# GpSimd computes four of the eight parts of the final sum of a transformer block, VectorE the other four

## The chip, the cores and the metric

The kernel runs on one core of one Trainium2 chip. The metric is the device time of one execution in microseconds (us), lower being better. The compute engines of a core are TensorE (PE), VectorE (DVE), ScalarE (ACT) and GpSimd (POOL); SyncE (SP) only issues DMAs here. They run their own instruction streams and are ordered by semaphores.

## The reference, cut to what matters

The input x has 2 x 1024 rows of 128 float32 numbers. The output is x plus causal attention of the normalised rows plus a mixture of experts, in which each row takes the two best of 16 experts:

```python
xn = _layernorm(x, axis=-1)
x = x + _L0_attn_ref(xn, Wk, bk, Wq, bq, Wv, bv) + _L0_ffn_ref(xn, Wr, br, W1, b1, W2, b2)
# inside _L0_ffn_ref
gate = jnp.sum(jax.nn.one_hot(topi, NUM_BANKS) * topv[..., None], axis=-2)
h = jax.nn.relu(jnp.einsum('bsd,edh->bseh', tensor, W1) + b1)
y = jnp.einsum('bseh,ehm->bsem', h, W2) + b2
out = jnp.einsum('bse,bsem->bsm', gate, y)
```

What concerns the change is the last sum: every output row is a partial result (x, attention and the gated b2) plus gate 0 times the first expert's vector plus gate 1 times the second's.

## The kernel before, in words

The 2048 rows are 16 tiles (NT) of 128 rows, one row for each partition. `xin` (128 x 16 x 128, float32, in SBUF) starts as x and collects the output in place. The stages, in the order of time:

1. Rows are normalised and the router picks two experts for each; GpSimd scatters the rows to DRAM, sorted by expert (L361), in 47 tiles (TILES). L363 is a memset of a scratch tile between these scatters.
2. Attention of tiles 0 to 12 (the last three, `LATE`, wait until the end). For each tile VectorE adds the causal mask and takes the row maximum (L621), ScalarE exponentiates (L433), TensorE transposes (L847) and multiplies with v (L867), and VectorE adds the result to `xin` (L640), which raises `o_read`.
3. The 47 expert tiles: TensorE's two layers (L970 to L972, L982), ScalarE's ReLU (L473), VectorE's rescale into `ybuf` (L701), and an indirect DMA from the GpSimd queue that scatters each result to `pairs_dram` (L369), two vectors for each row of the input.
4. SyncE waits until the 47 scatters have landed (L313) and loads `pairs_dram` back in eight parts (NYL = 8) of two tiles each (TYL = 2), 256 KB a part (L315). Meanwhile the attention of tiles 13, 14 and 15 runs.
5. VectorE finishes the attention, waits for `o_read` to be 16, and runs `combine(n)` for n from 0 to 7. Each part is four `scalar_tensor_tensor` instructions on 128 x 128 (L724), two tiles for k = 0, a wait on its own semaphore (`step`), and two tiles for k = 1: `xin` = `pairs` x gate + `xin`. Both tensors are in SBUF. The last one raises `res_done`.
6. SyncE waits for `res_done` to be n + 1, in the order of n, and sends part n of `xin` to the output, 128 KB (L319). When all eight have landed the kernel ends.

The `pairs` tile lies in the same SBUF memory as the tile that the trace calls `slots`, so the rows of the trace call it `slots`. GpSimd's stream before the change ends with the 47 scatters (L365 to L371).

In L724 the operand of the gate is one number for each partition, `gate[:, k, t:t + 1]`. In front of GpSimd's engine, `step` (L326) makes it wait on its own semaphore, as VectorE's does.

The functions around the change:

Of the kernel before, what the change touches and what calls it, by code (L numbers as in the profile page):

```python
# [5 lines left out]
ALU = mybir.AluOpType  # L6
# [12 lines left out]
def attention_and_top2_experts(nc, x, Wk, bk, Wq, bq, Wv, bv, Wr, br, W1, b1, W2, b2, out):  # L19
# [3 lines left out]
    K = 2  # L23
    NT = B * S // P
# [19 lines left out]
    NYL = 8  # L44
    TYL = NT // NYL
# [7 lines left out]
    with ExitStack() as ctx:  # L53
        def sb(name, shape, dt):
            return ctx.enter_context(nc.sbuf_tensor(name, shape, dt))

        def sem(name):
            return ctx.enter_context(nc.semaphore(name))

        xin = sb("xin", [P, NT, D], F32)  # L60
# [57 lines left out]
        gate = sb("gate", [P, K, NT], F32)  # L118
# [12 lines left out]
        pairs = flat_slots[:, 0:NT * K * D].rearrange("p (t k d) -> p t k d", k=K, d=D)  # L131
# [57 lines left out]
        pairs_in = [sem(f"pairs_in{n}") for n in range(NYL)]  # L189
# [51 lines left out]
        o_read = sem("o_read")  # L241
# [4 lines left out]
        relu_done = sem("relu_done")  # L246
        l2_done = sem("l2_done")
        y_done = sem("y_done")
        res_done = sem("res_done")

        x_v = x.rearrange("b (t p) d -> p (b t) d", p=P)
        out_v = out.rearrange("b (t p) d -> p (b t) d", p=P)
# [21 lines left out]
        @block.sync  # L274
        def _(sp):
            def load_x(g):
                sp.dma_start(xin[:, G * g:G * g + G, :], x_v[:, G * g:G * g + G, :]).then_inc(x_in[g], 16)

            load_x(0)
            load_x(1)  # L280
            sp.dma_start(wr[:, :], Wr).then_inc(router_in, 16)
            load_x(2)
            sp.dma_start(brb[:, :], br.rearrange("(a e) -> a e", a=1).broadcast_to([P, E])).then_inc(router_in, 16)
            load_x(3)
            for n, w in enumerate((Wq, Wk, Wv)):
                sp.dma_start(wqkv[:, n, :], w).then_inc(proj_in, 16)
            sp.dma_start(bqk[:, 0:1], bq.rearrange("(p a) -> p a", a=1)).then_inc(proj_in, 16)
            sp.dma_start(bqk[:, 1:2], bk.rearrange("(p a) -> p a", a=1)).then_inc(proj_in, 16)
            sp.dma_start(b1rows[0:E, :], b1).then_inc(b1_in, 16)
            sp.wait_ge(blank_made, 1)  # L290
            whole = TILES // NBL * NBL
            blank_i = blank.bitcast(I32)
            sp.dma_start(blank_v[:, 0:whole, :].rearrange("p (m n) c -> p m (n c)", n=NBL),
                         blank_i.rearrange("p n c -> p (n c)")[:, None, :].broadcast_to([P, TILES // NBL, NBL * ROW])
                         ).then_inc(blank_sent, 16)
            sp.dma_start(blank_v[:, whole:TILES, :], blank_i[:, 0:TILES - whole, :]).then_inc(blank_sent, 16)
            sp.dma_start(bvb[:, :], bv.rearrange("(a d) -> a d", a=1).broadcast_to([P, D])).then_inc(bias_in, 16)
            for n in range(NW):
                here = slice(WG * n, WG * n + WG)
                sp.dma_start(w1[:, here, :], w1_v[:, here, :]).then_inc(w1_in[n], 16)  # L300
            sp.dma_start(b2rows[0:E, :], b2).then_inc(b2_in, 16)
            for n in range(NW):
                here = slice(WG * n, WG * n + WG)
                sp.dma_start(w2[:, here, :], w2_v[:, here, :]).then_inc(w2_in[n], 16)

            sp.wait_ge(proj_done, 3 * NG)
            sp.wait_ge(gates_done, 1)
            sp.wait_ge(rows_sent, 16 * K * NT)
            for n, (a, z) in enumerate(zip(XG, XG[1:])):
                sp.dma_start(slots_i[:, a:z, :], slots_v[:, a:z, :]).then_inc(slots_in[n], 16)  # L310

            for n in range(NYB):
                sp.wait_ge(y_sent[n], 16 * len(range(n, TILES, NYB)))  # L313
            for n in range(NYL):
                sp.dma_start(pairs[:, TYL * n:TYL * n + TYL, :, :],  # L315
                             pairs_v[:, TYL * n:TYL * n + TYL, :, :]).then_inc(pairs_in[n], 16)
            for n in range(NYL):
                sp.wait_ge(res_done, n + 1)
                sp.dma_start(out_v[:, TYL * n:TYL * n + TYL, :], xin[:, TYL * n:TYL * n + TYL, :]).then_inc(out_sent, 16)  # L319
            sp.wait_ge(out_sent, 16 * NYL)  # L320

        @block.gpsimd
        def _(pool):
            made = [0]

            def step(ins):  # L326
                made[0] += 1
                ins.then_inc(pool_step, 1)
                pool.wait_ge(pool_step, made[0])

            pool.memset(epsc[:, :], EPS)
            pool.memset(blank, 0.0)
            step(pool.memset(ident[:, :], 0.0))
            pool.affine_select(out=ident[:, :], in_=ident[:, :], compare_op=ALU.not_equal, fill=1.0,
                               base=0, pattern=[[-1, P]], channel_multiplier=1).then_inc(ident_made, 1)
            pool.iota(blank.bitcast(I32)[:, :, D:D + 1], pattern=[[0, NBL], [0, 1]], base=LOST,
                      channel_multiplier=0).then_inc(blank_made, 1)
            pool.iota(rows_i[:, :, D:D + 1], pattern=[[K * P, NT], [0, 1]], base=0, channel_multiplier=K)
            step(pool.iota(expert_no_i[:, :], pattern=[[1, E]], base=0, channel_multiplier=0))
            pool.tensor_copy(expert_no[:, :], expert_no_i[:, :])  # L340
            pool.memset(ones[:, :], 1.0)
            pool.memset(keep[:, :, 1:NT], 1.0)
            pool.memset(keep[:, :, 0:1], 0.0)
            pool.memset(ones16[:, :], 1.0 / P)
            step(pool.memset(before[:, :], 1.0))
            pool.affine_select(out=before[:, :], in_=before[:, :], compare_op=ALU.is_gt, fill=0.0,
                               base=0, pattern=[[1, P]], channel_multiplier=-1)
            step(pool.iota(tileno_i[:, :], pattern=[[0, 1]], base=0, channel_multiplier=1))
            pool.tensor_copy(tileno[:, :], tileno_i[:, :]).then_inc(consts, 1)
            step(pool.memset(causal[:, :], 0.0))  # L350
            pool.affine_select(out=causal[:, S - P:], in_=causal[:, S - P:], compare_op=ALU.is_ge, fill=-HUGE,
                               base=0, pattern=[[-1, P]], channel_multiplier=1).then_inc(consts, 1)

            pool.wait_ge(blank_sent, 32)
            pool.wait_ge(xn_done, NG)
            pool.wait_ge(slotrow_done, 1)
            for k in range(K):
                if k == 1:
                    pool.wait_ge(slotrow_done, 2)
                for t in range(NT):  # L360
                    pool.indirect_dma_start(slots_dram, bass.IndirectOffsetOnAxis(ap=slotrow[:, k, t:t + 1], axis=0),  # L361
                                            rows_i[:, t, :], None).then_inc(rows_sent, 16)
                    step(pool.memset(tick[:, :], 0.0))  # L363

            for j in range(TILES):  # L365
                if j in XG:
                    pool.wait_ge(pair_done, XG.index(j) + 1)
                pool.wait_ge(y_done, j + 1)
                pool.indirect_dma_start(pairs_dram, bass.IndirectOffsetOnAxis(ap=pair[:, j:j + 1], axis=0),  # L369
                                        ybuf[:, j % NYB, :], None, bounds_check=NT * P * K - 1,  # L370
                                        oob_is_err=False).then_inc(y_sent[j % NYB], 16)  # L371

        @block.scalar
        def _(act):
# [105 lines left out]
        def _(dve):  # L480
            made = [0]

            def step(ins):
                made[0] += 1
                ins.then_inc(dve_step, 1)
                dve.wait_ge(dve_step, made[0])
# [233 lines left out]
            def combine(n):  # L720
                dve.wait_ge(pairs_in[n], 16)
                for k in range(K):
                    for t in range(TYL * n, TYL * n + TYL):
                        ins = dve.scalar_tensor_tensor(out=xin[:, t, :], in0=pairs[:, t, k, :],  # L724
                                                       scalar=gate[:, k, t:t + 1], in1=xin[:, t, :], op0=ALU.mult,
                                                       op1=ALU.add)
                    if k + 1 < K:
                        step(ins)
                ins.then_inc(res_done, 1)

            attention(NT - LATE, NT)
            dve.wait_ge(o_read, NT)
            for n in range(NYL):
                combine(n)

        @block.tensor
# [290 lines left out]
```

## Time and profile before

| what | value |
|---|---|
| median of 3 runs | 206.0 us (205.99 to 206.23) |
| the profiled execution, its own time | 205.87 us |
| its span, first to last instruction | 204.1 us |
| busy: PE, DVE, ACT, POOL | 165.2, 115.0, 113.3, 100.0 us |
| TensorE's mean granted clock | 0.915 |

The profiled execution has 1.77 us outside its span. Busy time is an average over stages with different limits; what a stage depends on is read from the chain of waits and from the timeline of its stretch. A line of the timeline has the start, the duration, the engine, the line of the kernel, the operation, output <- input, the shape (partitions x elements), the count, and in brackets the idle time before it with what ended it. Durations of single instructions overlap somewhat with their neighbours on an engine, so the distance between two starts can be shorter than one duration.

### The profile page before, as it was taken

What the parts mean: (1) busy time and instruction counts of PE and PEld (TensorE: products, weight loads), DVE (VectorE), ACT (ScalarE), POOL (GpSimd) and SP (SyncE); (2) the same over time, 40 slices, a digit from 0 to 9 for tenths busy, and PEclk for the clock granted to TensorE, in tenths of its full rate; (3) what the DMA queues carried; (4) which work ended last, traced back from release to release, by engine and by line L of the source; (5) the groups of instructions that cost most, each with busy time, mean ns of one, the idle gap of its engine ahead of it and who ended that gap; (6) DMA issues with size and microseconds to landing.
All of it is one profiled execution on the core that took longest, in us unless ns stands there. A gap on an engine that the chain in (4) does not pass through costs nothing.

```text
span 204.1 us, 4590 instructions
## 1 busy us (share of the span) xinstructions
PE 165.2 (81%) x1464; PEld 146.3 (72%) x1464; DVE 115.0 (56%) x429; ACT 113.3 (56%) x325; POOL 100.0 (49%) x133
## 2 busy tenths in 40 slices
PE   5777999588989879205999999999998999988600
PEld 5667448446688578104999999999998999947500
DVE  3717777666979754303676644454444344354595
ACT  0885279268889582001988666656666666536000
POOL 7000008888888888840155545555555455640000
PEclk9995599999999999555999999999999999999975
DMA  5899999921011101129901100000100000007533
GB/s 158 281 323 181 385 408 409 408 82 39 29 42 39 39 29 39 39 53 303 279 29 43 38 29 37 18 11 39 42 31 24 28 30 32 24 0 242 174 103 103
DMA packets 22102, 23.69 MB, mean 116 GB/s; under 512 B 2689, under 2 KB 15515, under 8 KB 22080
## 3 DMA queue, kind: packets, MB, share of 16 engines
q1 hardware_dynamic: 19552, 19.16, 30.2%
q0 software_dynamic: 2528, 4.24, 6.0%
q8 instruction: 13, 0.21, 0.4%
q14 instruction: 9, 0.07, 0.1%
HBM read 14.98 MB, written 9.39 MB: 119 GB/s over the span
## 4 chain that ended last, share of the span: by engine, by line
PE 49%; POOL 24%; DVE 9%; ACT 6%; issue 6%; DMA 4%; DVEq 0%; SPq 0%; POOLq 0%; ACTq 0%
PE pO L982 21%; POOL slots_dram L361 15%; POOL tick L363 8%; PE pS L970 6%; PE pS L972 5%; PE pS L971 5%; DVE xin L724 4%; ACT rows L385 3%; PE pS L765 3%; PE pT L940 3%; PE pO L867 2%; PE pS L832 1%; PE pO L757 1%; DMA slots<-slots_dram 1%; DMA xin<-in_L_attn_x 1%
## 5 line engine op out<-in xcount | busy, mean ns | idle before, releaser
L473 ACT ACTIVATE xT<-pS,b1t 128x128 f32<-128x128 f32 x188 | 53.6, 372 | 40.8 <-PE pS L972 40.8
L369 POOL DMA_INDIRECT pairs_dram<-ybuf,pair x47 | 46.2, 983 | 46.4 <-DVE ybuf L701 41.4
L982 PE MATMUL pO<-w,xT 128*128 x376 | 51.7, 282 | 0.0
L361 POOL DMA_INDIRECT slots_dram<-rows,slotrow x32 | 32.3, 1010 | 34.1 <-DVE slotrow L563 25.5
L982 PEld LDWEIGHTS pO<-w,xT 128*128 128x128 f32 x376 | 45.5, 192 | 0.0
L693 DVE CAST xT<-pT 128x128 f16<-128x128 f32 x47 | 13.7, 291 | 44.8 <-PE pT L940 43.9
L970 PE MATMUL pS<-xT,w1hi 128*128 128x128 f16 x188 | 35.0, 223 | 2.4 <-DVE xT L694 1.9
L971 PE MATMUL pS<-xT,w1hi 128*128 128x128 f16 x188 | 35.0, 223 | 0.0
L972 PE MATMUL pS<-xT,w 128*128 128x128 f16 x188 | 35.0, 223 | 0.0
L970 PEld LDWEIGHTS pS<-xT,w1hi 128*128 x188 | 21.6, 115 | 3.4 <-DVE xT L694 2.5
L971 PEld LDWEIGHTS pS<-xT,w1hi 128*128 x188 | 21.6, 115 | 0.1
L972 PEld LDWEIGHTS pS<-xT,w 128*128 x188 | 21.6, 115 | 0.0
L940 PE MATMUL pT<-ident,slots 128*128 128x128 f32 x47 | 13.2, 286 | 8.7 <-DMA slots<-slots_dram 8.7
L867 PEld LDWEIGHTS pO<-v,probsT 128*128 128x128 f32 x144 | 17.7, 192 | 3.0 <-issue 1.4
L867 PE MATMUL pO<-v,probsT 128*128 128x128 f32 x144 | 18.9, 279 | 1.1 <-DVE wscale L609 1.1
L433 ACT ACTIVATE probs<-pS,negm 128x128 f32<-128x128 f32 (+7 forms) x16 | 11.9, 742 | 12.4 <-DVE negm L621 12.4
L832 PE MATMUL pS<-kT,qT 128*128 128x512 f32 (+3 forms) x48 | 17.9, 489 | 0.8 <-DVE v L585 0.8
L701 DVE TENSOR_SCALAR ybuf<-pO,cf 128x128 f32<-128x128 f32 x47 | 16.1, 343 | 3.2 <-PE pO L982 3.1
L363 POOL MEMSET tick<- 128x512 f32 x32 | 17.3, 540 | 0.0
L847 PE MATMUL pT<-ident,probs 128*128 128x128 f32 x72 | 10.9, 279 | 5.0 <-ACT probs L433 5.0
L694 DVE TENSOR_TENSOR xT<-pT,xT 128x128 f16<-128x128 f32 x47 | 13.7, 292 | 1.6
L621 DVE CUSTOM_DVE_ANT_0 pS<-pS,causal 128x128 f32<-128x128 f32 (+7 forms) x16 | 12.1, 762 | 4.1 <-PE pS L832 4.1
(125 smaller groups left out, 233.4 us busy)
## 6 DMA issues: line engine op xcount, KB each, us to landing
w<-in_L_ffn_W SPq DMA_DIRECT2D x8, 1024.0 KB, 14.8
slots_dram<-slots SPq DMA_DIRECT2D x1, 2860.0 KB, 13.5
slots<-pairs_dram SPq DMA_DIRECT2D x8, 256.0 KB, 5.7
slots<-slots_dram SPq DMA_DIRECT2D x1, 1495.0 KB, 13.3
xin<-in_L_attn_x SPq DMA_DIRECT2D x4, 256.0 KB, 3.1
out<-xin SPq DMA_DIRECT2D x8, 128.0 KB, 1.8
slots<-slots_dram SPq DMA_DIRECT2D x1, 780.0 KB, 7.3
pairs_dram<-ybuf,pair POOLq DMA_INDIRECT x47
```

The lines of the kernel that those rows point to most:

```text
L361: pool.indirect_dma_start(slots_dram, bass.IndirectOffsetOnAxis(ap=slotrow[:, k, t:t + 1], axis=0), rows_i[:, t, :], None).then_inc(rows_s ...
L363: step(pool.memset(tick[:, :], 0.0))
L369: pool.indirect_dma_start(pairs_dram, bass.IndirectOffsetOnAxis(ap=pair[:, j:j + 1], axis=0), ybuf[:, j % NYB, :], None, bounds_check=NT * ...
L473: ins = nc.scalar.activation(hid[:, j % NHB, here], pA(j)[:, here], ACT.Relu, bias=b1t[:, c, j:j + 1])
L701: dve.tensor_scalar(ybuf[:, j % NYB, :], pO[j % 2][:, 0:D], cf[:, j:j + 1], None, ALU.mult).then_inc(y_done, 1)
L832: ins = pe.matmul(pS[t % 2][:, a:z], qT[:, t * P:(t + 1) * P], kT[:, at + a:at + z], start=True, stop=True)
L867: ins = pe.matmul(pO[t % 2][:, 0:D], probsT[t % 2][:, j // G, j % G * P:(j % G + 1) * P], v[:, t // TB * TB + j, :], start=(j == 0), stop= ...
L940: pe.transpose(pT[j % 2][:, 0:D], slots[:, j, 0:D], ident[:, :]).then_inc(xs_done, 1)
L970: pe.matmul(to, w_hi, x_hi, start=True, stop=False)
L971: pe.matmul(to, w_hi, x_lo, start=False, stop=False)
L972: ins = pe.matmul(to, w_lo, x_hi, start=False, stop=True)
L982: ins = pe.matmul(pO[r % 2][:, 0:D], hid[:, r % NHB, c * P:(c + 1) * P], second_weights(r, c), start=(c == 0), stop=(c == NCH - 1))
```

## The change

VectorE's `combine` runs for the odd parts only. The even parts are computed by GpSimd, after its last scatter: for a part it waits for the pairs and for `o_read` of the part's two tiles, multiplies four 128 x 128 blocks of `pairs` in place by their gates (`tensor_scalar`), adds the two halves (`tensor_tensor`, 128 x 256), and adds the sum to `xin` (`tensor_tensor`, 128 x 256). A wait on its own semaphore stands between the three steps. `res_done` becomes two semaphores, and SyncE waits for one or the other in the order of n. Indices of `o_read`: parts 0, 2, 4 and 6 need it at 2, 6, 10 and 14.

```diff
-        res_done = sem("res_done")
+        res_dve = sem("res_dve")
+        res_pool = sem("res_pool")
...
             for n in range(NYL):
-                sp.wait_ge(res_done, n + 1)
+                if n % 2:
+                    sp.wait_ge(res_dve, n // 2 + 1)
+                else:
+                    sp.wait_ge(res_pool, n // 2 + 1)
                 sp.dma_start(out_v[:, TYL * n:TYL * n + TYL, :], xin[:, TYL * n:TYL * n + TYL, :]).then_inc(out_sent, 16)
...
+            for n in range(0, NYL, 2):
+                pool.wait_ge(pairs_in[n], 16)
+                pool.wait_ge(o_read, min(TYL * n + TYL, NT))
+                for k in range(K):
+                    for t in range(TYL * n, TYL * n + TYL):
+                        ins = pool.tensor_scalar(pairs[:, t, k, :], pairs[:, t, k, :], gate[:, k, t:t + 1], None,
+                                                 ALU.mult)
+                step(ins)
+                step(pool.tensor_tensor(pairs[:, TYL * n:TYL * n + TYL, 0, :], pairs[:, TYL * n:TYL * n + TYL, 0, :],
+                                        pairs[:, TYL * n:TYL * n + TYL, 1, :], ALU.add))
+                pool.tensor_tensor(xin[:, TYL * n:TYL * n + TYL, :], xin[:, TYL * n:TYL * n + TYL, :],
+                                   pairs[:, TYL * n:TYL * n + TYL, 0, :], ALU.add).then_inc(res_pool, 1)
...
-                ins.then_inc(res_done, 1)
+                ins.then_inc(res_dve, 1)
 
             attention(NT - LATE, NT)
             dve.wait_ge(o_read, NT)
-            for n in range(NYL):
+            for n in range(1, NYL, 2):
                 combine(n)
```

## Rows read from the trace of the kernel before

**Rows 1.** The chain that ended last, 191 to 204 us: start, duration, what.

```profile
190.90 1.02 PE pO L867 x9
...
192.01 0.36 DVE xin L640
192.37 0.02 issue
192.39 0.63 DVE xin L724 x2
193.02 0.02 issue
193.04 1.15 DVE xin L724 x4
...
198.92 1.15 DVE xin L724 x4
...
201.27 0.35 DVE xin L724
201.62 0.26 DVEq L53
```

**Rows 2.** One line's instructions, L724: durations in ns, first and last start.

```profile
L724 DVE SCALAR_TENSOR_TENSOR xin<-slots,gate,xin x32: 346/346/352, 192.4 to 201.5; 128x128 f32<-128x128 f32 x32
```

**Rows 3.** One line's instructions, L319, the output's DMAs, and their landing.

```profile
L319 SPq DMA_DIRECT2D out<-xin x8: 372/372/378, 193.7 to 201.9; - x8
DMA to landing us min/median/max: 1.8/1.8/1.8
```

**Rows 4.** The timeline of SyncE's queue, 178 to 205 us.

```profile
183.02 5.15 SPq L315 DMA_DIRECT2D slots<-pairs_dram  x8
193.68 8.60 SPq L319 DMA_DIRECT2D out<-xin  x8
```

**Rows 5.** L315 in short stretches: single loads of parts 0, 2 and 7; parts 6 and 7.

```profile
L315 SPq DMA_DIRECT2D slots<-pairs_dram x1: 359/359/359, 183.0 to 183.0; - x1
DMA to landing us min/median/max: 2.7/2.7/2.7
...
L315 SPq DMA_DIRECT2D slots<-pairs_dram x1: 463/463/463, 183.9 to 183.9; - x1
...
DMA to landing us min/median/max: 5.4/5.4/5.4
...
L315 SPq DMA_DIRECT2D slots<-pairs_dram x1: 1674/1674/1674, 186.5 to 186.5; - x1
DMA to landing us min/median/max: 6.4/6.4/6.4
...
L315 SPq DMA_DIRECT2D slots<-pairs_dram x2: 469/1072/1674, 186.0 to 186.5; - x2
...
DMA to landing us min/median/max: 6.3/6.3/6.4
```

**Rows 6.** L640 in the late attention, tiles 13 to 15, 187 to 193 us.

```profile
189.20 0.34 DVE L640 SCALAR_TENSOR_TENSOR xin<-pO,rinv,xin 128x128 f32<-128x128 f32 x1
```

**Rows 7.** The timeline of POOL, its last scatter, and its first 6 us.

```profile
180.76 0.98 POOL L369 DMA_INDIRECT pairs_dram<-ybuf,pair  x1 [0.30 <-issue]
...
3.45 0.29 POOL L346 TENSOR_SCALAR_AFFINE_SELECT slots<-slots 128x128 f16<-128x128 f16 x1
3.70 0.12 POOL L348 IOTA tileno_i<- 128x1 int32 x1
```

**Rows 8.** Groups of instructions of POOL by line: busy us, mean ns | idle before.

```profile
L334 POOL TENSOR_SCALAR_AFFINE_SELECT ident<-ident 128x128 f32<-128x128 f32 x1 | 0.3, 282 | 0.2 <-POOL ident L333 0.2
L363 POOL MEMSET tick<- 128x512 f32 x32 | 17.3, 540 | 0.0
L341 POOL MEMSET ones<- 128x128 f32 x1 | 0.2, 198 | 0.0
```

**Rows 9.** Groups of instructions of DVE by line and shape.

```profile
L561 DVE TENSOR_TENSOR slots<-slots 128x256 f32<-128x256 f32 x2 | 0.8, 420 | 0.0
L520 DVE TENSOR_TENSOR slots<-expert_no,slots 128x128 f32<-128x128 f32 x4 | 1.0, 285 | 0.0
L615 DVE SCALAR_TENSOR_TENSOR w<-w,wscale,w1hi 128x512 f16<-128x512 f32 x16 | 11.8, 746 | 0.0
```

**Rows 10.** The timelines of DVE and of POOL around 45 us.

```profile
44.67 0.56 DVE L607 TENSOR_SCALAR expo<-expo 128x4 int32<-128x4 int32 x1
45.27 0.17 DVE L608 TENSOR_SCALAR pw<-expo 128x4 int32<-128x4 int32 x1
...
44.66 0.54 POOL L363 MEMSET tick<- 128x512 f32 x1
```

**Rows 11.** The timeline of DVE around L615, beside POOL's memsets and scatters.

```profile
54.66 0.79 DVE L615 SCALAR_TENSOR_TENSOR w<-w,wscale,w1hi 128x512 f16<-128x512 f32 x1
```

## The prediction, written before the change was timed

> **What bounds the kernel now.** I read the chain that ended last first. Its tail is not TensorE: PE's last product ends at 191.9 us, L640 adds it to `xin`, and from 192.39 to 201.88 the chain is nothing but L724 on VectorE, all 32 instructions with gaps of 0.02 us [rows 1]. One part of the sum takes 1.175 us: (201.88 + 0.02 - 192.39) / 8 = 1.19 with its own waits, and 1.15 + 0.02 = 1.17 from the lines of four instructions. One L724 lasts 0.346 us [rows 2], and four of them would be 1.38, so neighbours overlap by 0.05 each. Next I read what follows: the last output DMA is issued at 201.9 and lands 1.8 later [rows 3], and the span ends at 204.1, 2.2 us after that issue. So the end is the issue of the last output DMA plus 2.2, and that issue waits for the last part.
>
> Then I asked when the inputs of the parts are there. SyncE issues the eight loads of pairs from 183.02 on [rows 4]. Part 0 lands 2.7 after 183.0, at 185.7; part 2 at 183.9 + 5.4 = 189.3; part 6 at 186.0 + 6.3 = 192.3 and part 7 at 186.5 + 6.4 = 192.9 [rows 5]. The loads between land about 0.7 apart, part 4 at about 190.9. `o_read` reaches 14 when tile 13 is added, 189.20 + 0.34 = 189.5 [rows 6], which is before GpSimd can come to part 6, so no `o_read` holds GpSimd back. GpSimd's last scatter ends at 181.7 [rows 7], so GpSimd is free when part 0 lands.
>
> **What the change removes.** Four of eight parts leave VectorE: 4 x 1.175 = 4.70 us. If nothing disturbs it, VectorE does parts 1, 3, 5 and 7 from 192.39 to 197.09.
>
> **What it adds: a part on GpSimd.** The trace has no `tensor_scalar` and no `tensor_tensor` on POOL.
> - Four multiplications of 128 x 128. The nearest row is the affine select of the same 128 columns, one input and one output: 0.282 us [rows 8], with 0.25 from its start to the next instruction's [rows 7]. I take 3 x 0.25 + 0.28 = 1.03 us. Bounds: below, a memset of that size, 0.2 each; above, 0.5 each, since the multiplication also fetches a gate for each partition, which no row shows.
> - Two additions of 128 x 256 with two inputs. Below, VectorE's own 0.42 us for that shape [rows 9]; above, two memsets of 512 columns, 2 x 0.54 = 1.1 [rows 8]. From 128 to 512 columns the memset grows by (540 - 198) / 384 = 0.89 ns a column; 512 columns fetched are 0.46, and the fixed part of the affine select is 0.28 - 0.11 = 0.17, together 0.63. A memset neither fetches nor adds, so I take 0.7.
> - Two waits on its own semaphore and one on SyncE's data: between 0.07 and the 0.24 that stood in front of the affine select; 0.1 each [rows 8].
>
> One part: 1.03 + 2 x 0.7 + 3 x 0.1 = 2.7 us, with ends at 1.8 (0.7 + 0.84 + 0.2) and 4.4 (2.0 + 2.2 + 0.2).
>
> The Trainium skill (GPSIMD Engine Reference, section 3.1) gives about 2.6 cycles at 1.2 GHz an element for a two-input addition on GpSimd. By that 256 columns would be an estimated 0.55 us plus the dispatch, and the sum would not move by more than 0.2 us.
>
> **GpSimd's line without any disturbance.** Part 0 runs from 185.7 to 188.4; part 2 from its landing at 189.3 to 192.0; part 4 to 194.7; part 6 to 197.4. Two parts thus run while VectorE is still in the attention, and cost nothing there: in that stretch VectorE reads PSUM and at most one SBUF tensor (L621, L631, L640), and TensorE, which sets the end of the attention, doesn't wait on GpSimd. The other two run beside VectorE's four.
>
> **SyncE's queue.** It sends in the order of n. Part 0 goes at about 188.5, right after the last L315 has left the sequencer at 188.2 [rows 4]; then it stands waiting for part 1, which VectorE has at 193.6. Nothing else is in that queue. The 128 KB of part 0 may push the loads still in flight by about 0.4 us; part 4 is needed 1.1 after it lands and part 6 2.4 after, so this costs nothing. If parts 6 and 7 are ready together, the last DMA is issued 0.37 later, for the issue before it [rows 3]. I count 0.2.
>
> **Both engines on SBUF at once.** This is the term that decides. At 44.67 a VectorE instruction on 4 columns lasts 0.56 us, while its neighbour of the same kind takes 0.17; GpSimd's memset started at 44.66 and lasted 0.54 [rows 10]. It looks as if VectorE stood still for the whole of GpSimd's instruction. On the other hand L615, which like L724 reads two SBUF tensors, takes 0.73 to 0.79 us beside the same memsets (mean 0.746 [rows 9], for example [rows 11]), so it is not held up by a GpSimd instruction that only writes. No row has L724's kind beside a GpSimd instruction that reads.
>
> The Trainium skill (SBUF — State Buffer, section "Who interferes with whom") speaks against this change: a VectorE instruction with two SBUF inputs and a GpSimd instruction that reads SBUF exclude one another, and the second one is blocked until the first is done. The trace agrees as far as it goes, in that the 4-column instruction was blocked and L615 was not. By that rule taken to the letter the time would be that of the second rival below.
>
> In the shared stretch VectorE has 4.7 us of work, and GpSimd has 2 x 2.7 less what it did before 192.39, 5.0 us; 9.7 together. If they exclude each other only while data flow: VectorE grows by (420 - 285) / 128 = 1.05 ns a column [rows 9], 16 x 0.135 = 2.2 us; GpSimd has 8 x 0.11 + 4 x 0.46 = 2.7. That is half of 9.7 and leaves room, though each will often find the other in its way. I bound the cost by nothing (parts end at 197.4) and by all in turn (192.39 + 9.7 = 202.1, and 0.8 more if L724's overlap of 4 x 0.05 a part is lost as well, 202.9 at most) and take the middle: the last part is there at 200.0, its DMA is issued at 200.2, against 201.9 now. That is 1.7 us sooner.
>
> **The sum.** The profiled execution took 205.87 us, a span of 204.1 and 1.77 around it, 0.13 below the median of 206.0. 205.87 - 1.7 = 204.2, and against the median 206.0 - 1.7 = **204.3 us**.
>
> **The rivals.**
> - *The two engines don't disturb each other.* For it: L615 was not disturbed [rows 11]. Against it: [rows 10]. The last part is then part 6 at 197.4, and part 7 goes 0.4 later, at 197.8, 4.1 sooner than now: 201.9. With a GpSimd part at 1.8 VectorE's 197.1 would be last: 201.2.
> - *They take turns in full*, the rule above: everything from 192.39 on is one queue of 9.7 us, which ends at 202.1 instead of 201.88, or at 202.9, plus 0.2 for the output: 0.4 to 1.2 slower, 206.4 to 207.2, **slower**, say 206.8. It decides the sign once turns add more than about 4.5 us to the 197.4. For it speaks that a blocked VectorE instruction waited out the whole memset [rows 10]. In the profile L724 would show 0.5 to 1 us in place of 0.346.
> - *GpSimd is simply too slow.* With a part at 4.4 its parts would end at 190.1, 194.5, 198.9 and 203.3, and with the output's issue the kernel ends 1.8 later than now: 207.8, also slower. The point from which this decides is a part of (201.5 - 185.7) / 4 = 3.95 us. For it: no row shows either operation on POOL. Against it: the affine select is as fast as a VectorE instruction of that size.
>
> **How the numbers follow.** Partial disturbance, my forecast: 0.43, with a range of its own of 202.7 to 205.9. No disturbance: 0.17. Turns in full: 0.26. GpSimd too slow: 0.14. A measurement of this kernel can tell 0.2%, 0.4 us, from no change. Faster are the first case but for 0.03 at its upper end, all of the second and a little (0.04) of the others, where turns in full meet a cheap GpSimd part: 0.61. Within 0.4 us: the upper end of the first and the lower end of the third and fourth, 0.12. Slower: 0.27. The range that leaves out 2 in 10 goes from 201.4, which takes in most of the undisturbed case, to 207.2, the dear end of turns in full; the slow GpSimd beyond it is left out.
>
> **What the profile of the changed kernel would show.** POOL's `tensor_scalar` at 0.28 and `tensor_tensor` at 0.7 us; part 0 ready at 188.4 and part 2 at 192.0; before 192.4 everything on PE, ACT and DVE as now. After it, L724 longer than 0.346, by how much being the disturbance: 16 of them end at 197.1 if there is none, at 202 or later if turns are full. The last line of the chain may be VectorE or GpSimd. The forecast is wrong if L724 stays at 0.346, if the GpSimd instructions cost more than 0.5 and 1.1 us already before 192.4, where nothing disturbs them, or if PE's last product moves away from 191.9.

## The result, and the profile after

The changed kernel took **210.95 us** (median of 4 runs, 209.81 to 211.13) against 206.0 (205.96 to 206.23): ratio 1.0227, 95% interval 1.019 to 1.0263. That is 5 us slower; forecast were 1.7 us faster, in a range that ended at 207.2. The profiled execution took 210.95 us, with a span of 209.2 against 204.1, so the 5 us are in the span. Medians here are of all runs of a kernel, while the ratios leave out runs in a second, slower state of the chip, so the two need not agree to the last tenth.

First the part whose parts the prediction priced, the timeline of the changed kernel from 186 us on (GpSimd's and VectorE's lines of the sum, and SyncE's; L383, L386, L388 are GpSimd's three steps, L742 is the old L724, L658 the old L640, L323 the old L319):

```profile
186.03 2.35 POOL L383 TENSOR_SCALAR slots<-slots,gate 128x128 f32<-128x128 f32 x4 [4.08 <-DMA slots<-pairs_dram]
188.46 0.73 POOL L386 TENSOR_TENSOR slots<-slots 128x256 f32<-128x256 f32 x1
189.27 0.73 POOL L388 TENSOR_TENSOR xin<-xin,slots 128x256 f32<-128x256 f32 x1
189.98 2.34 POOL L383 TENSOR_SCALAR slots<-slots,gate 128x128 f32<-128x128 f32 x4
190.03 13.32 SPq L323 DMA_DIRECT2D out<-xin  x8
192.21 0.35 DVE L658 SCALAR_TENSOR_TENSOR xin<-pO,rinv,xin 128x128 f32<-128x128 f32 x1 [1.44 <-PE pO L885]
192.59 6.98 DVE L742 SCALAR_TENSOR_TENSOR xin<-slots,gate,xin 128x128 f32<-128x128 f32 x16
193.90 2.79 POOL L383 TENSOR_SCALAR slots<-slots,gate 128x128 f32<-128x128 f32 x4
...
198.34 2.48 POOL L383 TENSOR_SCALAR slots<-slots,gate 128x128 f32<-128x128 f32 x4
...
201.71 0.72 POOL L388 TENSOR_TENSOR xin<-xin,slots 128x256 f32<-128x256 f32 x1
```

A part on GpSimd takes 189.98 - 186.03 = 3.95 us where nothing disturbs it, not 2.7, and the cause is L383: four multiplications take 2.35 us, 0.6 each, where I had 1.03. Part 6 ends at 202.43. VectorE's four parts take 6.98 us, not 4.70, and end at 199.57. The last L658 starts 0.2 us later than L640 did before [rows 1]; this lag is there at 178 us already, before GpSimd's new work, so it is not the change's.

But this is not 5 us. The last output DMA is issued at 202.9 and lands by 204.8, one microsecond later than before [rows 3]:

```profile
L323 SPq DMA_DIRECT2D out<-xin x2: 373/421/469, 202.5 to 202.9; - x2
DMA to landing us min/median/max: 1.9/1.9/1.9
```

With the 2.2 us behind it the span would be 205.1. It is 209.2. What lies behind shows in the view of one line, L53, the line to which the end of the program is put down. Its rows of the kernel before, which I had not read (durations in ns, start in us):

```profile
L53 POOLq DRAIN  x1: 8523/8523/8523, 179.7 to 179.7; - x1
L53 DVEq DRAIN  x1: 651/651/651, 201.3 to 201.3; - x1
L53 SPq DRAIN  x1: 7/7/7, 203.9 to 203.9; - x1
```

and of the changed kernel:

```profile
L53 POOLq EVENT_SEMAPHORE  x2: 17/17/17, 209.0 to 209.1; - x2
L53 DVEq DRAIN  x1: 686/686/686, 198.9 to 198.9; - x1
L53 POOLq DRAIN  x1: 7300/7300/7300, 201.7 to 201.7; - x1
L53 SPq DRAIN  x1: 7/7/7, 205.0 to 205.0; - x1
```

Every engine's stream ends with a drain, and then all engines meet at a semaphore. VectorE's 0.65 us is the wait for its own last instruction. GpSimd's goes on for 209.0 - 202.43 = 6.6 us after its last instruction. It was just as long before: from the last scatter's end at 181.7 [rows 7] to 188.2, 6.5 us, in time when GpSimd had nothing to do. SyncE is done at 205.0 in the changed kernel and then waits; its own waits say so (us in total, times, longest; the trace names TensorE's queue, but TensorE's own drain began at 190.2 and took 2.0 us, and the only one that ends near 209.0 is GpSimd's):

```profile
SPq L53 <- PEq L53: 4.2, 1, 4.2
```

### The profile page after: what moved, and what is told of

Read it like the earlier page. It is cut to its first block, busy times and chain, and to the rows that moved or that the text cites. A ratio compares the mean times of both kernels' runs of the same rounds, so it can differ in the third digit from the quotient of the medians.

```text
span 209.2 us, 4602 instructions
## 1 busy us (share of the span) xinstructions
PE 169.0 (81%) x1464; PEld 149.0 (71%) x1464; DVE 113.4 (54%) x413; ACT 113.6 (54%) x325; POOL 115.2 (55%) x157
## 4 chain that ended last, share of the span: by engine, by line
PE 44%; POOL 30%; ACT 6%; DMA 6%; issue 6%; DVE 4%; POOLq 0%; SPq 0%; DVEq 0%; ACTq 0%
PE pO L1000 20%; POOL slots_dram L365 15%; POOL tick L367 8%; PE pS L988 6%; PE pS L990 5%; PE pS L989 5%; POOL slots L383 5%; ACT rows L403 3%; PE pS L783 3%; PE pT L958 3%; ACT xT L491 2%; PE pO L775 1%; DMA xin<-in_L_attn_x 1%; POOL slots L386 1%; DMA slots<-slots_dram 1%
## 5 line engine op out<-in xcount | busy, mean ns | idle before, releaser
L850 PE MATMUL pS<-kT,qT 128*128 128x512 f32 (+3 forms) x48 | 20.2, 541 | 0.8 <-DVE v L603 0.8
L639 DVE CUSTOM_DVE_ANT_0 pS<-pS,causal 128x128 f32<-128x128 f32 (+7 forms) x16 | 13.2, 827 | 4.9 <-PE pS L850 4.9
L865 PE MATMUL pT<-ident,probs 128*128 128x128 f32 x72 | 11.4, 285 | 5.2 <-ACT probs L451 5.2
L865 PEld LDWEIGHTS pT<-ident,probs 128*128 128x128 f32 x72 | 8.6, 146 | 8.7 <-ACT probs L451 7.5
```

What stands on the lines that cost most here:

```text
L850: ins = pe.matmul(pS[t % 2][:, a:z], qT[:, t * P:(t + 1) * P], kT[:, at + a:at + z], start=True, stop=True)
L865: ins = pe.transpose(pT[a // G][:, (j - a) * P:(j - a + 1) * P], probs[:, t % 2, j * P:(j + 1) * P], ident[:, :])
```

## The experiments

The theory after reading the two traces: the end is the later of two, the last output's issue plus 2.2 us, and GpSimd's end plus 6.5 to 6.6 us. The rival: the arithmetic's price and contention explain all of it. The ratios below are to the kernel before on the same chip. Where an interval is wide, I go by the traces.

**The drain alone.** Two kernels in which GpSimd does no part of the sum.

```diff
+            pool.wait_ge(res_done, NYL)
```

> The kernel before, with one line more: GpSimd's stream ends with a wait until VectorE has finished all eight parts; it executes nothing. Theory (the drain at the end of GpSimd's stream takes 6.5 us after GpSimd's stream comes to it, 201.7 to 209.0 in the changed kernel, hidden from 181.7 to 188.2 in the kernel before): if the drain's length doesn't depend on what came before it, it now starts at 201.9, ends at about 208.4, and the time is about 210.4, with no GpSimd arithmetic at all. Theory B (the drain is long because GpSimd has just executed something): the drain is short here, and the time stays within 0.3 us of 206.0. Rival (the changed kernel is slow only because of the arithmetic's cost and of contention): 206.0.

```diff
+            pool.wait_ge(res_done, NYL)
+            pool.memset(epsc[:, :], EPS)
```

> The kernel before, and at the end of GpSimd's stream the same wait and one memset of one column, about 0.1 us. Theory (drain after any last instruction): the drain runs from about 202.1 to 208.6, time 210.5. Theory B of the run before: also 210.5 here, and only here. Rival (arithmetic and contention): 206.0 to 206.2.

Measured: 211.19 us (ratio 1.0229, 1.017 to 1.0288) and 210.99 us (1.0266, 1.0198 to 1.0334). A wait that executes nothing, on a kernel otherwise untouched, costs as much as the whole change. The expectations were 210.4 and 210.5. The rows of L53 of the first:

```profile
L53 POOLq DRAIN  x1: 6600/6600/6600, 202.9 to 202.9; - x1
L53 SPq DRAIN  x1: 7/7/7, 205.0 to 205.0; - x1
```

VectorE's last instruction ended at 202.45 in this execution, 0.6 us later than in the kernel before; the drain ends at 209.5, 4.5 after SyncE is done. The rival falls, and so does theory B: GpSimd need not have executed anything just before.

**Fewer parts on GpSimd.** Two parts, then three.

```diff
-            for n in range(0, NYL, 2):
+            for n in (0, 2):
...
-            for n in range(1, NYL, 2):
+            for n in (1, 3, 4, 5, 6, 7):
```

> The changed kernel, with GpSimd doing parts 0 and 2 only and VectorE the other six. GpSimd's last addition should end at 193.9, beside at most two or three of VectorE's instructions. Theory (the end is the later of GpSimd's end + 6.6 and VectorE's end + 2.2): GpSimd gives 200.5; VectorE 192.5 + 6 x 1.18 + 0.8 of contention = 200.4, + 2.2 = 202.6; span 202.6, time about 204.4, faster than before by 1.6 us. Rival without the drain: the same here, since VectorE is last in both; but it would then have put the changed kernel at 206.5. If the drain were not fixed but grew with the number of GpSimd instructions, the time could only be lower still.

> As the run with parts 0 and 2 on GpSimd, with part 4 there as well; VectorE has 1, 3, 5, 6, 7. GpSimd's third part ends at 193.9 + 4.4 = 198.3. Theory (end of GpSimd + 6.6): span 204.9 to 205.0, time 206.8, slower than with two parts by about 2 us although VectorE is done sooner, and near the time before. Rival without the drain: VectorE ends at 192.4 + 5 x 1.18 + 1.7 of contention = 200.0, + 2.2 = 202.2, time 204.0, as fast as with two parts or faster.

Two parts: 204.87 us, ratio 0.9935 (0.9912 to 0.9958), **faster** than the kernel before by 0.65%, little but clear of the scatter. GpSimd ended at 193.8 and its drain at 200.4, before SyncE was done at 202.5:

```profile
L53 POOLq DRAIN  x1: 7302/7302/7302, 193.1 to 193.1; - x1
L53 SPq DRAIN  x1: 7/7/7, 202.5 to 202.5; - x1
```

Three parts: 209.85 us, ratio 1.0135 (1.0059 to 1.021), more than the 206.8 expected. In that profile the late attention came 2.7 us later than in the kernel before (VectorE's first instruction of the sum at 195.13), so only differences count: GpSimd's end at 201.11 and the span at 207.9, 6.8 apart, while VectorE had ended at 203.35 and SyncE at 205.4. From VectorE's first instruction of the sum to the end of the span it is 12.8 us, against 10.5 with two parts (192.29 to 202.8), 2.3 more, and the expectation had 2.3. One part more made it slower although VectorE had less to do, as the drain theory has it and the rival doesn't.

**Who holds whom up.** GpSimd's six instructions of a part became memsets of 512 columns; the gated sum of parts 0, 2, 4 and 6 is left out.

```diff
-                        ins = pool.tensor_scalar(pairs[:, t, k, :], pairs[:, t, k, :], gate[:, k, t:t + 1], None,
-                                                 ALU.mult)
+                    ins = pool.memset(w1[:, (n * 3 + k) % E, :], 0.0)
```

> The changed kernel with GpSimd's six instructions a part replaced by six memsets of 512 columns into a tensor that is no longer needed. It leaves out the gated sum of parts 0, 2, 4 and 6. Theory (VectorE's two-input instruction is held up only by a GpSimd instruction that reads SBUF): the 16 instructions of VectorE's combine are all at 0.346 us again, from 192.4 to 197.1, although GpSimd works beside them. Rival (any GpSimd instruction holds VectorE up): they still take up to 0.88 us, and four parts 6 to 7 us in all. GpSimd's end is at 185.9 + 4 x 3.1 = 198.5 or so, and by the drain theory the span is 205.1 and the time 206.9.

Measured: 206.97 us, one run, as the drain theory asked: GpSimd ended at 198.4, SyncE was done at 200.9, and the span was 205.1. One line's instructions, first in this kernel, then in the changed one: all 16 of L742, those of 193.9 to 196.6 (beside four multiplications; the 876 is one that began beside L388), those of 197.64 to 198.3 (begun beside L386 and beside L388), and the four multiplications.

```profile
L738 DVE SCALAR_TENSOR_TENSOR xin<-slots,gate,xin x16: 346/347/353, 192.6 to 197.1; 128x128 f32<-128x128 f32 x16
```

```profile
L742 DVE SCALAR_TENSOR_TENSOR xin<-slots,gate,xin x16: 340/371/876, 192.6 to 199.2; 128x128 f32<-128x128 f32 x16
...
L742 DVE SCALAR_TENSOR_TENSOR xin<-slots,gate,xin x9: 340/358/876, 193.2 to 196.1; 128x128 f32<-128x128 f32 x9
...
L742 DVE SCALAR_TENSOR_TENSOR xin<-slots,gate,xin x2: 809/842/876, 196.9 to 197.6; 128x128 f32<-128x128 f32 x2
...
L383 POOL TENSOR_SCALAR slots<-slots,gate x4: 638/682/847, 193.9 to 196.0; 128x128 f32<-128x128 f32 x4
```

Beside instructions that only write, VectorE's 16 are at 0.347, undisturbed. In the changed kernel it is a matter of which GpSimd instruction runs: beside the two-input additions L386 and L388 (0.73 us each) a VectorE instruction lasts 0.67 to 0.88, four of the 16, which is 1.9 of the 2.3 us; the other twelve, most of them beside the one-input multiplications, stay at 0.34 to 0.45, and it is GpSimd that is slowed, from 0.60 to 0.64 to 0.85. So beside one kind VectorE waits the addition out, and beside the other hardly at all. Whether the number of inputs makes the difference is not shown: the two kinds differ in operation and size as well, and no run takes these apart. The rule of the Trainium skill (SBUF — State Buffer, "Who interferes with whom"), by which a two-input VectorE instruction and a GpSimd instruction that reads SBUF exclude one another while one that only writes is no matter, fits the memsets and the additions; beside the multiplications the trace shows much less than that on VectorE's side.

**A cheaper part.** One broadcast multiplication in place of four with a scalar for each partition.

```diff
-                        ins = pool.tensor_scalar(pairs[:, t, k, :], pairs[:, t, k, :], gate[:, k, t:t + 1], None,
-                                                 ALU.mult)
-                step(ins)
+                step(pool.tensor_tensor(pairs[:, TYL * n:TYL * n + TYL, :, :], pairs[:, TYL * n:TYL * n + TYL, :, :],
+                                        gate[:, :, TYL * n:TYL * n + TYL].rearrange("p k t -> p t k")[:, :, :, None]
+                                        .broadcast_to([P, TYL, K, D]), ALU.mult))
```

> The changed kernel with GpSimd's four tensor_scalar of a part (4 x 0.6 us) replaced by one tensor_tensor on 128 x 512 with the gates broadcast along the row. If it costs 1.3 us (0.73 for 256 columns plus 0.55 for 256 more), a part takes 2.9 us, and GpSimd's end comes at 198.2 plus 0.8 of contention, 199.0. Drain theory: span 205.6, time 207.5, 3.4 us less than the changed kernel, all of it from GpSimd's earlier end. Rival (contention decides): two-input instructions hold VectorE up for longer than tensor_scalar did, so VectorE would end later than in the changed kernel and the time would stay at 210 or above.

Measured: 207.72 us, ratio 0.9994 (0.9935 to 1.0054), against 1.0227 for the change. The profiled execution was the fastest of ten, 205.02 us, so by the ratios the gain is 2.3%, 4.8 us, and less than its span says. The timeline of GpSimd in it:

```profile
185.50 1.05 POOL L381 TENSOR_TENSOR slots<-slots,gate 128x512 f32<-128x512 f32 x1 [4.01 <-DMA slots<-pairs_dram]
186.63 0.73 POOL L384 TENSOR_TENSOR slots<-slots 128x256 f32<-128x256 f32 x1
...
195.69 0.72 POOL L386 TENSOR_TENSOR xin<-xin,slots 128x256 f32<-128x256 f32 x1
```

512 columns in one instruction take 1.05 us where four times 128 took 2.35. GpSimd ends at 196.4, 2.6 sooner than expected, its drain at 203.0, and the span is 203.2, with SyncE done at 201.6. GpSimd's end came 6.0 us sooner than in the changed kernel (0.5 of it because this execution's loads landed that much sooner), and the span shrank by 6.0, the drain's distance staying as it was. The rival of this run (VectorE held up longer) was half right: VectorE's 16 took 7.53 us, up from 6.98, but VectorE didn't set the end.

**What makes the drain long.** Small kernels that leave out the whole computation: SyncE loads x and stores it as the output, and GpSimd issues 0, 1, 20 or 79 DMAs (79 is what the large kernels issue, 32 + 47) and waits for them.

```diff
+            for n in range(N):
+                pool.indirect_dma_start(rows_dram, bass.IndirectOffsetOnAxis(ap=idx[:, n:n + 1], axis=0),
+                                        tick[:, 0:D], None).then_inc(told, 16)
+            pool.wait_ge(told, 16 * N)
```

> A kernel that leaves out the whole computation: SyncE loads x and stores it as the output; GpSimd executes one memset of 512 columns and waits for the load. GpSimd issues no DMA. Theory A (the drain at the end of GpSimd's stream has a fixed length): 6.5 us here too. Theory B (it is the price of having issued DMAs from GpSimd): under 1 us, like VectorE's 0.65 and ScalarE's 0.61. I think A and B equally likely.

> The same small kernel, with one DMA of 256 KB issued by GpSimd and waited for before the end. Both theories expect a drain of 6.5 us; if it is long here and short in the kernel without that DMA, B holds.

> The small kernel (no computation, x stored as the output) with one indirect scatter DMA of 128 rows issued by GpSimd. Theory C (one indirect DMA is enough, whose code on GpSimd makes the later drain long): 6.5 us. Theory D (the drain grows with the number of DMAs that GpSimd has issued; 79 in the large kernels, 6.5 / 79 = 0.08 us each): 0.1 to 0.2 us. Theory E (something else in the large kernels): 0.1 us.

> The same with 20 scatters of 128 rows. C: 6.5 us. D: 20 x 0.08 = 1.7 us. E: 0.1 us.

> The same with 79 scatters, as many as the large kernels have (32 + 47). C and D: 6.5 us. E: 0.1 us, in which case the cause of the drain's length stays open.

> The same with 79 plain DMAs of 64 KB from GpSimd and no indirect one. If the length belongs to any DMA issued by GpSimd and grows with their number (D), 6.5 us; if it needs indirect ones, 0.1 to 0.2 us, as after the single plain DMA before (0.135 us).

GpSimd's last drain, from the view of its line, in these kernels (one run each; 14.34, 14.82, 14.16, 32.02, 111.56 and 53.9 us):

| DMAs issued by GpSimd | its drain, us |
|---|---|
| none | 0.041 |
| 1 plain | 0.135 |
| 1 indirect | 0.133 |
| 20 indirect | 1.693 |
| 79 indirect | 6.517 |
| 79 plain | 6.517 |

The rows of 20 and of 79 scatters:

```profile
L25 POOLq DRAIN  x1: 1693/1693/1693, 28.3 to 28.3; - x1
```

```profile
L25 POOLq DRAIN  x1: 6517/6517/6517, 103.0 to 103.0; - x1
```

(1.693 - 0.133) / 19 = 0.082 us and (6.517 - 0.133) / 78 = 0.082 us: **a straight line in the number of DMAs that GpSimd has issued**, whatever their kind, although all had landed before the drain began. Theory D holds; C (a fixed price) and E fall. Of the first two expectations, A falls with the 0.041 us, and B, as I had put it, with the 0.135: one DMA is not enough. It is not their size: the one plain DMA moved 256 KB and the one scatter 64 KB, at the same price. Nor is it the instructions: after 79 DMAs the drain takes 6.5 us with 85 GpSimd instructions in the small kernel and with 133 in the kernel before. All these DMAs have 128 rows, so a price for each DMA and a price for each row are not told apart. Why a landed DMA still costs the drain 82 ns stays open.

**Can the debt be paid early?** The changed kernel with drains in GpSimd's idle time.

```diff
                     step(pool.memset(tick[:, :], 0.0))
+            pool.drain()
...
                                         oob_is_err=False).then_inc(y_sent[j % NYB], 16)
+                if j % 12 == 11 or j == TILES - 1:
+                    pool.drain()
```

> The changed kernel with five drains added to GpSimd's stream: one after the 32 row scatters (GpSimd is idle there anyway), one after every 12th expert scatter and one after the last. The question is whether the 0.082 us for each GpSimd DMA is owed since the start of the kernel, or since the last drain. Theory D1 (since the last drain): the drains take 2.6, 1.0, 1.0, 1.0 and 0.9 us, all in idle time, the last one from 181.7 to 182.7, before part 0's data is there; the final drain takes 0.1 us. The end is then the output of part 6: GpSimd ends at 202.4, the last output DMA is issued at 202.9, span 205.1, time 206.9 against about 211 for the changed kernel. Theory D2 (a drain always pays for all DMAs so far): the drains take 2.6, 3.6, 4.6, 5.6 and 6.5 us, the last of them holds part 0 up until 188.2, and the time is 213 or more.

Measured: 206.61 us, ratio 1.0052 (1.0028 to 1.0076). By the ratios that is 1.7%, 3.6 us, less than the change without them; the spans are 204.8 and 209.2. Its drains:

```profile
L368 POOLq DRAIN  x1: 2678/2678/2678, 89.1 to 89.1; - x1
L378 POOLq DRAIN  x4: 2987/3100/3606, 120.4 to 179.4; - x4
L53 POOLq DRAIN  x1: 836/836/836, 201.3 to 201.3; - x1
```

The first pays for 32 DMAs, 32 x 0.082 = 2.6 us. The four later ones last 2.99, 2.99, 3.21 and 3.61 us with the scatters that they stand behind; from the end of the scatter before them it is 1.8, 1.8, 2.0 and 1.6 us. They don't grow with the DMAs issued in all: each pays only since the one before. But they are 0.6 to 0.9 us longer than the 1.0 that 11 or 12 DMAs should cost, and the cause of that stays open. The last drain ends at 202.2, 0.1 us after GpSimd's last addition. Theory D1 holds, its 1.0 us apart. What is left of the change then is 1.0 us slower than before, the arithmetic and contention.

**Versions meant to be faster.** VectorE has two idle stretches in the late attention, which the profile shows as its waits for TensorE (1.88 us before the copy of tile 15, 1.44 before the last L658). In four kernels it does two of its parts there; the diff is that of the one with parts 0 and 2 on GpSimd, the others differ in the numbers of the parts, and the last has the early drains and the one multiplication as well.

```diff
                     inverse_sum(t)
+                    if t == NT - 2:
+                        combine(1)
                     if t + 1 < z:
                         probsT_copy(t + 1)
                     if t > a:
                         attended(t - 1)
+                    if t == NT - 1:
+                        combine(3)
```

> GpSimd does parts 0 and 2; VectorE does part 1 in its idle stretch after the reciprocal of tile 14 and part 3 in the one after it has added tile 14, and 4, 5, 6, 7 at the end. Theory: GpSimd ends at 193.9, its drain at 200.5; VectorE 192.4 + 4.7 + 0.9 of contention = 198.0, + 2.2 = 200.2. Span 200.6, time 202.4, if the two parts delay none of TensorE's products. Rival (the parts in the gaps are late, or held up by GpSimd, and push the copy of the transposed probabilities and so TensorE): PE's last product after 192.2, time 203.5 or more.

> GpSimd does part 0 alone; VectorE parts 1 and 2 in the same two idle stretches and 3 to 7 at the end. GpSimd ends at 190.0 and its drain at 196.6, hidden. VectorE 192.4 + 5 x 1.18 = 198.3 without contention, + 2.2 = 200.5. Span 200.5, time 202.3: the same as with two parts on GpSimd, within 0.3 us. If contention near 192.3 to 193.9 is dearer than I reckon, this one is the faster.

> The kernel before with VectorE doing parts 0 and 1 in its two idle stretches of the late attention and 2 to 7 at the end; GpSimd does no part. VectorE ends at 192.4 + 6 x 1.18 = 199.5, + 2.2 = 201.7 span, against 204.1 before: 2.4 us faster, ratio 0.988. That is one part (1.2 us) slower than with part 0 on GpSimd. If the gaps were not free, PE's last product would come later than in the kernel before.

> The changed kernel unaltered, for its ratio on the same chip as the runs beside it: 1.02 to 1.027. The drain should again start at GpSimd's end and last 6.5 to 6.6 us from there.

> Everything that the runs taught, in one: the early drains, one multiplication of 128 x 512 a part on GpSimd, parts 0, 2 and 4 there, parts 1 and 3 in VectorE's two idle stretches of the late attention, and 5, 6, 7 at the end. GpSimd ends at 194.1 and owes 0.1 us; VectorE 192.4 + 3 x 1.18 + 0.9 of contention = 196.8, + 2.2 = 199.0 span, time 200.8, ratio to the kernel before 0.975. What could spoil it: GpSimd's two-input instructions, 0.73 and 1.05 us long, hold VectorE up in the first idle stretch (1.9 us for a part of 1.2), which would delay the copy for TensorE and the whole tail by up to 0.5 us. Without the early drains the end would be at 194.1 + 6.5 = 200.6 span, 202.4.

| kernel | us, median | ratio to before, 95% |
|---|---|---|
| gaps, two parts on GpSimd | 204.52 | 0.9822 (0.9736 to 0.9908) |
| gaps, part 0 on GpSimd | 204.06 | 0.9825 (0.9753 to 0.9897) |
| gaps, VectorE alone | 203.96 | 0.9869 (0.9811 to 0.9928) |
| gaps, three parts, one multiplication, early drains | 202.17 | 0.9802 (0.9776 to 0.9827) |
| the change, beside "VectorE alone" | 211.23 | 1.0203 (1.0142 to 1.0263) |

The medians belong to different chips; the ratios are to be compared. VectorE's idle time alone is worth 1.3%, with TensorE undisturbed: its spans were 202.1 (expected 201.7), 200.9 with part 0 on GpSimd (200.5) and 201.0 with two parts (200.6). With two parts it is again GpSimd's drain that ends last, at 200.8 against SyncE's 200.2. GpSimd adds some 0.5% to that, within the intervals. When the changed kernel was run again beside these, its drain ended 6.6 us after GpSimd's last addition, as the first time. The last version has the lowest ratio, though the intervals overlap and it is 0.5% short of its 0.975. The profiled execution was its slowest, 203.0 us, so what its timeline of VectorE shows need not hold for the others:

```profile
186.43 2.21 DVE L666 SCALAR_TENSOR_TENSOR xin<-slots,gate,xin 128x128 f32<-128x128 f32 x4
...
191.23 3.17 DVE L666 SCALAR_TENSOR_TENSOR xin<-slots,gate,xin 128x128 f32<-128x128 f32 x4 [0.85 <-DMA slots<-pairs_dram]
194.33 0.34 DVE L659 SCALAR_TENSOR_TENSOR xin<-pO,rinv,xin 128x128 f32<-128x128 f32 x1
194.70 4.30 DVE L666 SCALAR_TENSOR_TENSOR xin<-slots,gate,xin 128x128 f32<-128x128 f32 x12
```

A part in the first idle stretch took 2.2 us, held up by GpSimd's two-input instructions, where it took 1.24 and 1.37 beside the one-input ones and 1.25 with none. The copy followed at 188.56, 1.30 us after the first of TensorE's transposes that it waits for, against 1.13 in the kernel before (187.46 to 188.59): 0.2 us late. The second one waited for a load that landed late in this execution, at 191.2, then took 3.17 beside GpSimd, and put the last three parts off to 194.7. I had feared the first stretch, and in this execution the time went in the second. Why the load was late is not shown. GpSimd's drain was no matter any more (it ended at 195.9).

## Why the prediction was wrong

- **The step that failed: "the end is the issue of the last output DMA plus 2.2, and that issue waits for the last part".** I read the end as SyncE's alone. There is a second path, GpSimd's last work plus a drain of 6.5 us, 0.082 for each of 79 DMAs. It ended at 188.2 in the kernel before, hidden by 16 us. The change put GpSimd's last work at 202.4, and the drain at 209.0. It makes 4.1 of the 5.1 us of span (205.1 to 209.2), and the runs with a mere wait, with fewer parts and with early drains all bear it out. No rival of mine had it. I had noted that GpSimd's last scatter ends at 181.7 and never asked what comes after it in the stream.
- **The second term that was mis-sized: GpSimd's multiplication**, 0.25 to 0.28 us from the affine select, "above, 0.5 each". It takes 0.60 undisturbed, above my upper bound, and already before 192.4, which I had named as a sign that the forecast is wrong. The addition at 0.7 was right (0.73). A part cost 3.95 us in place of 2.7, exactly the point at which I had said that a slow GpSimd decides the sign. Without the drain this rival would have won, with the span 1.0 us longer; the run with early drains, 0.5% slower than before, is close to that case. So the sign was wrong for this reason too, and the drain only made it worse. (The bounds of a part were also added up loosely: four times 0.2 is 0.8, not 0.7, and the upper end of 4.4 has the cheap waits, with 0.24 each it is 4.9.)
- **Contention was over-sized on the path that ended last.** I took the middle between none and full turns, which moved the last part from 197.4 to 200.0, 2.6 us. VectorE did lose 2.3 us, but its last part, at 199.57, was not the last: GpSimd's was, and GpSimd lost only 0.6 us over two parts. That VectorE's end fell near 200.0 is luck. Its form was other, too: L742 waits out a two-input addition or is hardly touched.
- **The forecast's own sum, redone.** The last output was to be issued at 200.2 and was at 202.9, 2.7 us later: +4.4 because four GpSimd parts from 186.03 on end at 201.8 and not 197.4, -2.0 for contention (0.6 in place of 2.6), +0.3 for two outputs in a row (0.5 in place of 0.2). The drain's 4.1 come on top: 6.8 in all, from a span of 202.4 to 209.2. One error hid part of another.
- **Right:** parts 0 and 2 cost nothing in the attention (TensorE's products were as long as before), SyncE's order and the loads cost nothing but the pair at the end, and `o_read` held nothing back.
- Against the kernel before: +0.2 us because this execution's tail was that much later, +0.35 because part 6 ends later than part 7 did, +0.45 for two outputs in a row, +4.1 for the drain: 5.1.

## What to carry to other kernels

Ask of each engine that a change gives late work, not only how long the work takes, but what the engine still owes at the end of its stream; look at the drains and semaphores of the program's last line for all engines, also where they cost nothing today. If GpSimd has issued many DMAs, either leave its stream finished early, or drain it in idle time before it gets late work. And price a GpSimd instruction by its own kind: one broadcast `tensor_tensor` of 512 columns (1.05 us) was cheaper than two `tensor_scalar` of 128 (1.2).

## What the runs showed of the hardware that I had not expected

- GpSimd's drain lasts about 0.05 + 0.082 us x (DMAs of 128 rows it has issued since its last drain): 0.041, 0.133, 1.693 and 6.517 us after 0, 1, 20 and 79, with all of them landed, and 2.68 after 32. Drains directly behind a scatter took 0.6 to 0.9 more. The Trainium skill (VectorE: DVE Perf Modes, "The DRAIN you can't avoid") calls the drains at a kernel's ends constant, about 12 ns on all engines; here that held for the other four engines in the small kernels (8 to 13 ns), not for GpSimd.
- GpSimd's `tensor_scalar` with a scalar for each partition takes 0.60 us for 128 columns, its `tensor_tensor` 0.73 for 256 and 1.05 for 512 with a broadcast input; a line through these two, an estimate from unlike instructions, is 0.41 us plus 1.25 ns a column.
- A VectorE instruction with two SBUF inputs waits out GpSimd's two-input instruction (0.346 becomes 0.67 to 0.88 beside 0.73 us, and up to 1.13 beside the 1.05 us one), is not slowed by memsets (0.347), and hardly by GpSimd's `tensor_scalar` (0.34 to 0.45).
